# Windowed-attention layers: transposed probabilities placed by transfers instead of engine copies, rotated keys finished ahead of the row sums, and a new order of GpSimd's work

## What is computed

```
qkv = shift_tokens(x) @ Wqkv[i];  q, k, v = split into 16 heads of 64
q = l2norm(q) * q_scale;  k = l2norm(k) * k_scale          # rows of 64
q, k = rotary with a position scale (q * s, k / s)
bk2, bv2 = each window of 32 keys / values with the 32 before it
sim = einsum(q, bk2) * 8, masked;  attn = softmax(sim)      # 32 queries x 64 keys
x = (attn @ bv2) @ Wo[i] + x
x = gated MLP (layer norm, W1, gelu, W2) of shift_tokens(x) + x
```

## Time and profile before

| what | value |
|---|---|
| median of 3 runs | 3153.22 us (3150.84 to 3154.32) |
| the profiled execution | 3146.83 us, span 3144.8 us |
| PE, DVE, ACT, POOL busy, share of the span | 88%, 78%, 67%, 43% |
| first to last row maximum of the local layers (L1568) | 896.7 to 2695.7 us |
| mean granted TensorE clock | 0.954 of full speed |

### The profile page before, as it was taken

How to read it: one execution, slowest core, us unless ns; L and a number is a source line. 1 busy time by engine, 2 the same in 40 slices (tenths; PEclk the granted TensorE clock), 3 DMA queues, 4 the chain that set the end, 5 groups by cost and what they waited for, 6 DMA issues and landing times. The chain is left out here.

```text
span 3144.8 us, 72108 instructions
## 1 busy us (share of the span) xinstructions
PE 2774.6 (88%) x27244; PEld 1692.0 (54%) x27244; DVE 2442.2 (78%) x3071; ACT 2104.3 (67%) x3079; POOL 1351.6 (43%) x1209
## 2 busy tenths in 40 slices
PE   5799999997678989888889898989999999789997
PEld 3122222223546565656566666656665656478885
DVE  3899999992379797979798888888888979455554
ACT  2488888885158787878788787878787878311111
POOL 1000000000078685867586758676766767200000
PEclk7799999998589999999999999999999999889998
DMA  3011111100010001000100010001000000000001
GB/s 131 27 29 28 28 29 29 29 24 8 8 57 9 6 9 43 7 8 9 42 9 6 17 34 9 8 15 36 8 7 14 15 7 9 12 18 0 0 0 34
DMA packets 56465, 64.35 MB, mean 20 GB/s; under 512 B 24742, under 2 KB 38964, under 8 KB 55348
## 3 DMA queue, kind: packets, MB, share of 16 engines
q1 hardware_dynamic: 55380, 60.58, 7.0%
q10 hardware_dynamic: 864, 0.79, 0.1%
HBM read 36.69 MB, written 7.34 MB: 14 GB/s over the span
## 5 line engine op out<-in xcount | busy, mean ns | idle before, releaser
L886 DVE TENSOR_REDUCE a_minus_max<-a_ps_max 128x1 f32<-128x1024 f32 x512 | 596.8, 1218 | 57.6 <-PE a_ps_max L811 52.3
L794 ACT ACTIVATE a_expT<-a_ps_scoresT 128x512 f32<-128x512 f32 (+1 forms) x683 | 528.8, 808 | 78.2 <-PE a_ps_scoresT L829 67.4
L1178 POOL TENSOR_TENSOR b_turned_q<-b_rot_q,b_turned_q 128x1024 f32<-128x1024 f32 x96 | 226.8, 2362 | 270.2 <-DVE b_turned_q L1549 257.3
L844 PE MATMUL a_ps_out<-a_expT,v_aug 128*32 128x256 f32 x4096 | 327.9, 392 | 5.4 <-ACT a_outT L781 4.8
L1620 DVE STREAM_TRANSPOSE b_probsT<-b_probs 32x512 f32<-32x512 f32 x384 | 269.4, 702 | 11.9 <-POOL b_probs L1219 0.3
L765 POOL CAST a_max_hi<-a_minus_max 128x16 bf16<-128x16 f32 x32 | 6.3, 198 | 631.1 <-DVE a_minus_max L886 631.1
L1287 ACT ACTIVATE b_kT<-b_psD 64x512 f32<-64x512 f32 x384 | 226.1, 589 | 58.6 <-PE b_psD L1374 53.5
L829 PE MATMUL a_ps_scoresT<-a_q_op,a_k_op 26*128 26x512 bf16 x1024 | 247.2, 385 | 13.1 <-ACT a_expT L794 4.4
L1225 POOL TENSOR_TENSOR b_turned_k<-b_rot_k,b_turned_k 128x512 f32<-128x512 f32 x192 | 243.9, 1270 | 0.2 <-DVE b_turned_k L1549 0.2
L1185 POOL TENSOR_TENSOR b_rot_q<-b_turned_q,b_inv_norm 128x1024 f32<-128x1024 f32 x96 | 182.8, 1904 | 137.7 <-issue 137.7
L1219 POOL TENSOR_TENSOR b_probs<-b_probs,b_inv_sum 128x512 f32<-128x512 f32 x192 | 197.3, 1049 | 99.1 <-DVE b_inv_sum L1593 99.1
(11 more groups left out here) (295 smaller groups left out, 6019.4 us busy)
## 6 DMA issues: line engine op xcount, KB each, us to landing
b_v_edge<-b_v SPq DMA_DIRECT2D x96, 128.0 KB
b_w_qkv<-L_ffn_Wqkv SPq DMA_DIRECT2D x6, 1536.0 KB
a_q_op<-terms_q SPq DMA_DIRECT2D x128, 48.0 KB
a_k_op<-terms_k SPq DMA_DIRECT2D x128, 48.0 KB
joined<-a_outT SPq DMA_DIRECT2D x256, 16.0 KB
b_w_o<-L_ffn_Wo SPq DMA_DIRECT2D x6, 512.0 KB
a_q_op<-a_max_rows SPq DMA_DIRECT2D x128, 4.0 KB
b_w<-L_ffn_W SPq DMA_DIRECT2D x6, 341.0 KB
```

The lines of the kernel that those rows point to most:

```text
L794: act.activation(expT[:, to:to + 512 * size], ps_scoresT[:, at:at + 512 * size], ACT.Exp, scale=SCALE_A).then_inc(exp_ready, 1)
L844: last_mm = pe.matmul(ps_out[lo:lo + 32, 256 * part:256 * part + 256], v_aug[:, b * T8 + kt, head, :], expT[:, at:at + 256], start=(kt == ...
L886: dve.tensor_reduce(minus_max[p % 2][:, side, 0, qt:qt + 1], ps_max[u % 2][:], AX.X, ALU.max, negate=True).then_inc(max_taken, 1)
L1178: pool.tensor_tensor(turned[:], rot[:], turned[:], ALU.add).then_inc(added, 1)
```

## The change

1. The own part is transposed like the other one, by a single DVE instruction into a new tile `packed_own`. `probsT` is laid out as [keys, window, head, 32], so that each window's block is one run of 2 KB per partition.
2. Eight transfers a step, issued by SP, place the blocks: four from `packed` (`back_placed`) and four from `packed_own` (`own_placed`). The copies by ACT and GpSimd and the tile `ones` are gone. PE and DVE wait for the two new semaphores instead.
3. DVE multiplies the keys by the sine table ahead of the row sums instead of behind them.
4. GpSimd's order in a step is: queries, first half of the keys, both products of the normalisation, second half of the keys.
5. PE puts the band matmuls (the mask) between the two halves of the key transposes.
6. `w_qkv` of the next layer comes in six transfers of 256 KB, one behind each step s = 2 to 7 of the first batch.

```diff
-        probsT = sb("probsT", [P, HEADS_B, P])
+        packed_own = sb("packed_own", [P, HEADS_B, W])
+        probsT = sb("probsT", [P, P // W, HEADS_B, W])
...
@@ SP, step @@
                     sp.dma_start(v_edge[par][P - W:P, :], v[1 - par][P - W:P, :]).then_inc(v_edge_in, 16)
+                if 1 in lags:
+                    sp.wait_ge(packed_ready, T)
+                    if 2 in lags:
+                        sp.wait_ge(out_half, 2 * (T - 1))
+                    sp.dma_start(edgeT[P - W:P], packed[0:W]).then_inc(back_placed, 16)
+                    for j in range(1, P // W):
+                        sp.dma_start(probsT[W * j - W:W * j, j], packed[W * j:W * j + W]).then_inc(back_placed, 16)
+                    sp.wait_ge(packed_own_ready, T)
+                    for j in range(P // W):
+                        sp.dma_start(probsT[W * j:W * j + W, j], packed_own[W * j:W * j + W]).then_inc(own_placed, 16)
+                if b == 0 and not isinstance(s, int) and not (isinstance(l, int) and l == LAST):
+                    load_qkv_part(l + 1, (l + 1) % 2, s - 2)
...
@@ GpSimd, step @@
-                    for j in (2, 3):
-                        rows = slice(W * j, W * j + W)
-                        pool.tensor_tensor(probsT[W * j - W:W * j, :, rows], packed[rows], ones[rows].unsqueeze(2).to_broadcast([W, HEADS_B, W]),
-                                           ALU.mult).then_inc(high_back_ready, 1)
...
+                if 0 in lags:
+                    unit_keys(0)
                 if 1 in lags:
+                    normalise(0)
+                if 1 in lags:
+                    normalise(1)
                 if 0 in lags:
+                    unit_keys(1)
...
@@ ACT, step @@
-                    act.activation(edgeT[P - W:P], packed[0:W], ACT.Copy).then_inc(low_back_ready, 1)
-                    act.activation(probsT[0:W, :, W:2 * W], packed[W:2 * W], ACT.Copy).then_inc(low_back_ready, 1)
...
@@ PE, step @@
-                    turn(rot_k, unit_k_ready, 2, qT_held, kT_half)
+                    turn(rot_k, unit_k_ready, 2, qT_held, kT_half, (0,))
...
+                    turn(rot_k, unit_k_ready, 2, qT_held, kT_half, (1,))
...
-                    pe.wait_ge(probsT_ready, 4 * (T - 1))
-                    pe.wait_ge(low_back_ready, 2 * (T - 1))
-                    pe.wait_ge(high_back_ready, 2 * (T - 1))
+                    pe.wait_ge(own_placed, 64 * (T - 1))
+                    pe.wait_ge(back_placed, 64 * (T - 1))
...
@@ DVE, step @@
+                if 0 in lags:
+                    rotary_sin(psK, turned_k, parts_k_ready, 2)
                 if 1 in lags:
                     dve.wait_ge(exp_ready, T)
...
-                if 0 in lags:
-                    rotary_sin(psK, turned_k, parts_k_ready, 2)
...
-                    for j in range(P // W):
-                        rows = slice(W * j, W * j + W)
-                        dve.transpose(probsT[rows, :, rows], probs[rows, :, 1, :]).then_inc(probsT_ready, 1)
-                        if j == 0 and ahead:
-                            scale(ahead[0], ahead[1], 0)
+                    if 2 in lags:
+                        dve.wait_ge(own_placed, 64 * (T - 1))
+                    dve.transpose(packed_own[:], probs[:, :, 1, :]).then_inc(packed_own_ready, 1)
+                    if ahead:
+                        scale(ahead[0], ahead[1], 0)
```

More of the change, by code:

```diff
@@ L1007, in local_blocks @@
         packed_ready = sem("packed_ready")
-        probsT_ready = sem("probsT_ready")
-        low_back_ready = sem("low_back_ready")
-        high_back_ready = sem("high_back_ready")
+        packed_own_ready = sem("packed_own_ready")
+        back_placed = sem("back_placed")
+        own_placed = sem("own_placed")
         out_half = sem("out_half")
@@ L1084, in load_qkv, with load_qkv_part @@
                 sp.dma_start(w_qkv[:, ds(at, 3 * INNER)], wts["Wqkv"][ds(l, 1)].rearrange("o p n -> p (o n)")).then_inc(w_qkv_in, 16)
+            def load_qkv_part(l, slot, part):
+                at = slot * 3 * INNER + part * 512
+                sp.dma_start(w_qkv[:, ds(at, 512)], wts["Wqkv"][ds(l, 1), :, ds(part * 512, 512)].rearrange("o p n -> p (o n)")).then_inc(w_qkv_in, 16)
             def load_o(l):
@@ L1139, in _ @@
             load_mlp(0)
+            sp.wait_ge(zeroed, 9)
             stream(sp, step, middle)
@@ L1214, in step, with unit_keys @@
                     unit(rot_q, turned_q, sum_q_ready, unit_q_ready, qT_half, 0)
+                def unit_keys(half):
+                    heads = slice(8 * half, 8 * half + 8)
+                    pool.wait_ge(parts_k_ready, 2 * T + 2)
+                    pool.tensor_tensor(turned_k[:, heads], rot_k[:, heads], turned_k[:, heads], ALU.add).then_inc(sum_k_ready, 1)
+                    pool.wait_ge(sum_k_ready, 2 * T + half + 1)
+                    pool.wait_ge(inv_norm_ready, T + 1)
+                    pool.wait_ge(kT_half, 2 * T)
+                    pool.tensor_tensor(rot_k[:, heads], turned_k[:, heads],
+                                       inv_norm[:, HEADS_B + 8 * half:HEADS_B + 8 * half + 8].unsqueeze(2).to_broadcast([P, 8, DH]),
+                                       ALU.mult).then_inc(unit_k_ready, 1)
@@ L1215, in step, with normalise @@
+                def normalise(c):
+                    pool.wait_ge(inv_sum_ready, T)
+                    pool.tensor_tensor(probs[:, :, c, :], probs[:, :, c, :],
+                                       inv_sum[:].unsqueeze(2).to_broadcast([P, HEADS_B, W]), ALU.mult).then_inc(probs_ready, 1)
+                if 0 in lags:
+                    unit_keys(0)
                 if 1 in lags:
-                    pool.wait_ge(inv_sum_ready, T)
-                    for c in range(2):
-                        pool.tensor_tensor(probs[:, :, c, :], probs[:, :, c, :],
-                                           inv_sum[:].unsqueeze(2).to_broadcast([P, HEADS_B, W]), ALU.mult).then_inc(probs_ready, 1)
+                    normalise(0)
@@ L1221, in step @@
+                if 1 in lags:
+                    normalise(1)
                 if 0 in lags:
-                    pool.wait_ge(parts_k_ready, 2 * T + 2)
-                    for half in range(2):
-                        heads = slice(8 * half, 8 * half + 8)
-                        pool.tensor_tensor(turned_k[:, heads], rot_k[:, heads], turned_k[:, heads], ALU.add).then_inc(sum_k_ready, 1)
-                        pool.wait_ge(sum_k_ready, 2 * T + half + 1)
-                        pool.wait_ge(inv_norm_ready, T + 1)
-                        pool.wait_ge(kT_half, 2 * T)
-                        pool.tensor_tensor(rot_k[:, heads], turned_k[:, heads],
-                                           inv_norm[:, HEADS_B + 8 * half:HEADS_B + 8 * half + 8].unsqueeze(2).to_broadcast([P, 8, DH]),
-                                           ALU.mult).then_inc(unit_k_ready, 1)
+                    unit_keys(1)
@@ L1363, in step, with turn @@
                 if isinstance(s, int) and s == 0 and b == 0 and 0 in lags:
-                    pe.wait_ge(w_qkv_in, 16 * (l + 1))
+                    pe.wait_ge(w_qkv_in, 16 + 16 * 6 * l)
                 w_at = l % 2 * 3 * INNER
-                def turn(src, unit, parts, held, done):
-                    for half in range(2):
+                def turn(src, unit, parts, held, done, halves=(0, 1)):
+                    for half in halves:
                         pe.wait_ge(unit, parts * (T - 1) + half % parts + 1)
@@ L1434, in step @@
                                 at = P * (pair % 4)
-                                pe.matmul(psD[half][rows, at:at + P], v[par][:, DH * head:DH * head + DH], probsT[:, head, :],
+                                pe.matmul(psD[half][rows, at:at + P].rearrange("p (j w) -> p j w", w=W), v[par][:, DH * head:DH * head + DH], probsT[:, :, head, :],
                                           start=(pair % 4 == 0), stop=False, skip_group_check=True)
@@ L1514, in _ @@
         def _(dve):
-            dve.wait_ge(zeroed, 10)
+            dve.wait_ge(zeroed, 9)
             def centre(l, b, n):
```

30 lines of the change are left out of this document (7 added, 23 removed).

## The result

The changed kernel takes 3185.83 us, median of 3 runs (3185.5 to 3189.67), against 3153.22 before: a ratio of 1.0109 (95% interval 1.0086 to 1.0131). It is slower by 33 us where 33 us less were forecast. The profiled execution took 3185.5 us, its span is 3183.3 us.

What follows compares the result with a forecast made beforehand. It took a closed route through GpSimd, PE, ACT and DVE, 15.94 us a step, as the bound. With 15.45 a step, 41.2 us less and 7.7 more gave 3153.2 - 33 = 3120 us, range 3102 to 3166.

Steps and rivals of the forecast that it cites:

- I take 0.55 a transfer: SP's eight placing transfers: issue price taken from `v_edge`; last issued 4.4 us after `packed`, landing at 5.7.
- The price of `joined`: Alternative transfer price from the group of eight to `joined`: 5.30 us for eight issues, landing 1.3 later, 6.6 in all.
- The route itself: From the product with the values through keys, scores, `packed` and transfers to a later such product: 30.9 us over two steps.
- key route: Closed route through GpSimd's keys, PE's transposes and scores, and DVE: from 15.94 us a step to 15.33.
- rival 1: Transfers cost what `joined` costs: step 15.9 us, 3158 us in all, about no change; chance 0.15.
- The gain of 41 us on plain steps: 84 steps without an MLP, each falling from 15.94 to 15.45 us: 41.2 us less.
- the forecast's term of 5.4 us: Steps with `ahead`, where the MLP's layer norm begins: `scaled` 0.45 us later, over twelve MLPs.
- rival 3: Transfers go one after the other, 1.8 us each, 14.5 for eight: step 19.85, 3490 us; chance 0.04.
- Rival 4: GpSimd, still at the queries, does the keys' first half too late, gain gone: about 3160 us; chance 0.07.
- Rival 2: Slower through SP's queue, nine transfers a step in place of one: for instance 3212 us; chance 0.13.
- threshold of 6.5: Last transfer landing later than 6.5 us after `packed` makes the kernel slower; there plain steps just pay for 7.7 us.
- price of 42 us for each us: Each us that the transfers land later costs 0.5 us a step, 42 us in all.

Runs made afterwards that it cites:

- e1: Changed kernel without the last two own placing transfers, six a step in place of eight, output wrong there: 3131.51 us, ratio 0.9947.
- e2: Changed kernel with two more transfers of the same size a step, into a tile nobody reads: 3293.55 us, ratio 1.0448.
- e6: Changed kernel with six transfers; GpSimd places two back windows behind the second half of the keys, nothing left out: 3124.09 us, ratio 0.9929.
- e8: Changed kernel with one of the eight transfers, a back window, issued by ACT ahead of squaring the keys: 3155.12 us, ratio 1.0026.
- e10: e6 with two extra PE products nobody reads behind `spread`, in steps where an MLP's layer norm begins: 3111.62 us, ratio 0.9887.
- e12: Kernel before the change with one extra PE product behind `spread`, in steps where an MLP's layer norm begins: 3139.14 us, ratio 0.9976.
- e3: Changed kernel with DVE's sine product of the keys ahead of the layer norm's centring, where an MLP's layer norm begins: 3183.16 us, ratio 1.0102.
- e4: Changed kernel with transfers kept but the old order on DVE, GpSimd and PE: 3147.19 us, ratio 1.0006.
- e9: e6 with `scaled` ahead of the own transpose, in steps where an MLP's layer norm begins: 3113.39 us, ratio 0.9884.
- e5: Kernel before the change with the new order alone on DVE, GpSimd and PE, no placing transfers: 3296.83 us, ratio 1.0476.
- e7: Changed kernel with two own transfers issued by GpSimd behind the keys, the other six by SP: 3136.88 us, ratio 0.9976.

## Why the prediction was wrong

**The step that failed** is "I take 0.55 a transfer, because the number of partitions is the same". Measured: 0.51, then 0.62 for each that follows another one, 5.06 us from `packed` to the end of the eighth issue (forecast 4.4), and 1.61 to PE's start (forecast 1.4 with the wake-up): 6.67 for 5.8. The price of `joined`, in the same group of rows, was the right one in its sum (5.30 + 1.3 = 6.6), though it has 8 partitions; its parts were off both ways (0.66 an issue for 0.62, and 1.3 for 1.61), so that the sum fits is in part luck. `v_edge` stood alone; nothing in its row said what a transfer takes with another in front of it.

**The route itself held.** Its other pieces were 25.05 us in the rows above and 25.1 in the forecast, and it goes round in two steps; e1, e2, e6 and e8 moved the step by about half of what the landing moved, as far down as the key route allows. With 6.67 it gives 15.86: rival 1's step of 15.9. The gain of 41 us on plain steps shrank to 84 x 0.08 = 7, and ten steps of 17 to 19 us took these back, some 14 us above 16.4 by this estimate. Each of the ten follows a tile in which an own transfer landed late, 2.7 to 3.7 us after its issue, beside an `instruction` packet; in three of them the clock fell as well. The forecast had no such term. So the 84 plain intervals sum up to 1352 us, before 1351. The forecast had taken all 84 of the kernel before as 15.94 (1339 us); four of them are 17.8 to 20.2.

**The `ahead` steps: a mechanism was missing.** In time, `scaled` came 0.4 us later than before, as forecast (0.45). But the forecast's term of 5.4 us counted these steps as if the product with the values were on time there. In 5 of 11 it was late, and `scaled` another 1.8 to 4.1 us later, 13 us in all; each of these five, too, follows a tile with an own transfer that landed late (2.8 to 3.4 us). And more MLPs began at the lower clock level, at some 1.5 us each (3.45 for 1.95, more in two of them): 9 us more than before, in these two executions. The three make 27 us by this estimate; the 11 intervals with an MLP grew by 26.5 us, where 5 were forecast. With that rival 1's time of 3158 becomes some 3180; the rest to 3186 stays open.

**What held.** The key route of 15.33 (e1, and every second step); GpSimd's first half of the keys directly behind the sine product (1788.05 to 1788.13); issues follow each other without waiting for landings, so rival 3 is out: each transfer as a rule lands 2.0 us after its issue, and the next issue comes after 0.62. The Trainium skill's rule that is cited there ("DMA: Bandwidth & Descriptors", "Rules for kernel authors"), that such transfers serialise, is not borne out as a wait of one for the other; that small ones pay mostly overhead is, as issue time. Rival 4 was not seen. The last tile's product now waits 8.67 us in place of 5.78, but the end came no later.

**Rival 2** had the right side and the right queue. Its threshold of 6.5 was passed by a little, and its price of 42 us for each us was too low: e2, 1.25 us later, has a ratio larger by 0.034 than the changed kernel's, 107 us. The price left out the MLPs (e2's intervals with one sum up to 28 us more than the changed kernel's) and the clock (164 us at the lower level for 58).

**Still open** is which of PE's waits lets the clock fall. Of the MLPs between row maxima, those with a wait of 0.5 to 0.83 us ahead of their first product never began at the lower level (0 of 33, in e10 to e12). With 1.68 or 1.69 us, 25 of 44 did (5 in the kernel before, 6 in e3, 8 in e4, 6 in e9), and with 1.9 to 2.4 us 65 of 77 (the changed kernel, e1, e2, e5 to e8). One length can go both ways: in e6 one MLP kept the clock after a wait of 2.36 us (its first two products took 1.96) and another lost it after 2.37 (3.75). The Trainium skill ("TensorE: Matmul & The Clock Gate", "Why this matters for your kernels") advises against idle gaps between bursts; e10 and e12 agree with it and tell no bound. Open, too, is why a transfer lands late beside an `instruction` packet.

## What to carry to other kernels

Price a row of transfers by a row of transfers: a lone one does not show what the next in the queue costs. When work leaves busy engines for a queue, follow the route from the last landing back to itself, over as many steps as it takes, and then look what the late consumer does where the pattern is broken (here the MLPs). Where a queue's issue time is the price, two items fewer or a second queue can decide (1.0109 became 0.9929 in e6 and 0.9976 in e7). And look at what else moves on the DMA queues when a transfer lands late.

## What the runs showed of the hardware

- 64 KB between partitions of SBUF: 0.51 us to issue alone, 0.62 behind another; 1.9 to 2.0 us from issue to landing as a rule. Beside a packet of the queues called `instruction`, the slowest of four took 2.4 to 3.7 us in 22 of 25 tiles. The 2.0 agrees with the fixed cost of about 2 us in the Trainium skill ("DMA: Bandwidth & Descriptors", "Anatomy of one DMA"), which the page gives for transfers that GpSimd issues; these are SP's.
- GpSimd issued such a transfer in 0.52 us, ACT in 0.54 and beside a running instruction.
- A wait of 1.7 to 2.4 us on PE can cost it twice: the wait, and then work at half the clock (two products took 3.45 us for 1.95). Two products that nobody reads, in the wait, were worth 0.4% here.
